# Last steps and end of a decoder layer redone: another drain order, norm and quantisation per token tile, FFN in two batches, rounding on GpSimd

## The reference, cut to what matters

```
x = x + ssm(layernorm(x))            # in projection, causal convolution, selective scan
                                     # with 128 heads in 8 groups, gate, group norm, out projection
x = x + matmul(fake_quant(layernorm(x), x1_scale, x1_zp),
               fake_quant(ctx, x2_scale, x2_zp))     # per sequence, 256 x 512 by 512 x 512
t = layernorm(x)[:, perm]            # FFN: features permuted
t = einsum('bhd,hdm->bhm', t, up)    # 16 heads, 32 -> 128
t = gelu(t)
t = einsum('bhm,hmd->bhd', t, down)  # 128 -> 32
x = x + t[:, unperm]
fake_quant(x, s, z) = (clip(round(x / s + z), 0, 255) - z) * s
```

## Time and profile before

| What | us |
|---|---|
| median of 3 runs (839.54 to 2028.73) | 841.23 |
| the profiled execution | 838.24 |
| its span in the trace | 836.4 |
| PE busy | 786.0 (94%) |
| VectorE (DVE) busy | 719.7 (86%) |
| GpSimd (POOL) busy | 589.6 (70%) |
| ScalarE (ACT) busy | 543.2 (65%) |
| share of PE in the chain that ended last | 88% |

### The profile page before, as it was taken

How to read it: one execution, slowest core, us unless ns; L and a number is a source line. 1 busy time by engine, 2 the same in 40 slices (tenths; PEclk the granted TensorE clock), 3 DMA queues, 4 the chain that set the end, 5 groups by cost and what they waited for, 6 DMA issues and landing times.

```text
span 836.4 us, 14376 instructions
## 1 busy us (share of the span) xinstructions
PE 786.0 (94%) x4212; PEld 613.4 (73%) x4212; DVE 719.7 (86%) x924; ACT 543.2 (65%) x1129; POOL 589.6 (70%) x487
## 2 busy tenths in 40 slices
PE   3765999999999999999999999999999989998987
PEld 2554777887787778777788878777888778776554
DVE  6767898999899989999898989898999999799663
ACT  2437677677667766776766776666677677885333
POOL 3436887778887877788787877887778877684100
PEclk9987999999999999999999999999999999999899
DMA  4253434444344344433434444433444444531001
GB/s 162 76 182 116 165 112 157 157 165 152 138 151 151 112 150 163 163 137 110 157 135 163 150 150 163 158 110 121 163 163 150 134 150 157 177 101 38 1 1 51
DMA packets 44049, 111.12 MB, mean 133 GB/s; under 512 B 5748, under 2 KB 6644, under 8 KB 44020
## 3 DMA queue, kind: packets, MB, share of 16 engines
q1 hardware_dynamic: 44020, 110.76, 38.5%
HBM read 109.30 MB, written 1.44 MB: 132 GB/s over the span
## 4 chain that ended last, share of the span: by engine, by line
PE 88%; DVE 5%; issue 3%; ACT 2%; POOL 1%; DMA 1%; SPq 0%; ACTq 0%; DVEq 0%; POOLq 0%
PE ps_in L1237 16%; PE ps_in L1239 15%; PE ps_in L1238 15%; PE ps_y L1348 7%; PE ps_o L1237 7%; PE ps_o L1239 7%; PE ps_o L1238 7%; PE ps_t L1310 3%; PE ps_y L1351 3%; PE ps_t L1322 1%; PE ps_o L1530 1%; POOL res L556 1%; PE ps_t L1360 1%; PE ps_o L1514 1%; DMA res<-in_x 1%
## 5 line engine op out<-in xcount | busy, mean ns | idle before, releaser
L510 POOL TENSOR_TENSOR w_lo<-raw,w_hi 128x512 fp32r<-128x512 f32 x144 | 231.5, 1629 | 135.7 <-ACT w_hi L625 126.5
L1237 PE MATMUL ps_in<-h_hi,w_hi 128*128 128x512 f32 x560 | 226.0, 404 | 0.0
L1239 PE MATMUL ps_in<-h_hi,w_lo 128*128 128x512 f32 x560 | 219.2, 392 | 0.0
L1238 PE MATMUL ps_in<-h_lo,w_hi 128*128 128x512 f32 x560 | 217.8, 389 | 0.0
L680 ACT ACTIVATE e<-e,nag 128x256 f32<-128x256 f32 (+1 forms) x512 | 183.5, 444 | 6.4 <-POOL e L530 6.4
L948 DVE SCALAR_TENSOR_TENSOR hid<-ps_in,curc,hid 128x510 f32<-128x510 f32 x186 | 138.3, 743 | 5.9 <-ACT hid L645 1.5
L1237 PEld LDWEIGHTS ps_in<-h_hi,w_hi 128*128 128x128 f32 x560 | 105.0, 187 | 30.2 <-issue 10.6
L645 ACT ACTIVATE hid<-ps_in,curc 128x512 f32<-128x512 f32 x62 | 48.2, 777 | 116.1 <-PE ps_in L1239 116.1
L1239 PEld LDWEIGHTS ps_in<-h_hi,w_lo 128*128 128x128 f32 x560 | 105.1, 188 | 23.4
L1238 PEld LDWEIGHTS ps_in<-h_lo,w_hi 128*128 128x128 f32 x560 | 105.3, 188 | 20.4
L541 POOL TENSOR_TENSOR e<-e,gm 128x512 f32<-128x512 f32 x64 | 100.9, 1576 | 25.1 <-DVE gm L990 25.0
(11 more groups left out here) (234 smaller groups left out, 1240.6 us busy)
## 6 DMA issues: line engine op xcount, KB each, us to landing
e<-acs_rows SPq DMA_DIRECT2D x64, 768.0 KB, 4.5
raw<-in_w_in SPq DMA_DIRECT2D x144, 256.0 KB, 4.7
rawo<-in_w_out SPq DMA_DIRECT2D x64, 256.0 KB, 4.0
craw<-in_ctx SPq DMA_DIRECT2D x8, 256.0 KB, 2.6
res<-in_x SPq DMA_DIRECT2D x4, 256.0 KB, 3.2
out_x<-res SPq DMA_DIRECT2D x4, 256.0 KB, 2.2
acs_rows<-z SPq DMA_DIRECT2D x3, 128.0 KB, 2.9
rawo<-in_w_dt SPq DMA_DIRECT2D x1, 256.0 KB, 4.9
```

The costliest lines, as they stand in the source:

```text
L510: pool.tensor_tensor(w_lo[:, slot, :], raw[:, slot, :], w_hi[:, slot, :].bitcast(F32), ALU.subtract).then_inc(s_lo, 1)
L1237: pe.matmul(dst, lh, rh, start=first, stop=False)
L1238: pe.matmul(dst, lh, rl, start=False, stop=False)
L1239: return pe.matmul(dst, ll, rh, start=False, stop=last)
```

## The change

Nothing is changed ahead of the last group of heads.

- The context tiles are rounded by GpSimd in place of VectorE, in the last group's steps behind `mask_rows`, the last one in the drain.
- Drain: ScalarE does the gate tanh of a tile ahead of the exponentials, and the last gate tanh ahead of the last context scale and keep and of the split of `up`; VectorE gates the last tile ahead of all `one_hot`; the token sums stand ahead of the last but one output tile; GpSimd's group root stands ahead of the low half of `up`.
- Norm and quantisation go per token tile: variance, power, scale and offset of one tile at a time. The scale comes out of the power by itself (the variance is multiplied by the squared quantisation scale first). Rounding is one operation, and the turned tile is float, made bf16 by ScalarE with a bias (`keep_turned`).
- 6 fillers stay of 38. The column products stand in two pairs.
- From the product on the two sequences are separate batches: features, take, up, down and put back in halves of 256 tokens, with the second batch's norm and product between the first one's steps. High halves of the down product are ScalarE's. The row terms are added in the last operation (`finish`) in place of four by ScalarE.
- The table for Gelu is loaded behind the first split of features.

Most removed lines of the stages behind the drain stand in the functions printed above and are left out here, as are helpers that repeat the form of another.

```diff
-WARM_A, WARM_B = 18, 20
+WARM_A = 6
...
-        q1 = e_flat[:, 4:6, :].rearrange("p a n -> p (a n)").bitcast(BF16).rearrange("p (t d) -> p t d", t=TT)
...
+        def turn_bank(t):
+            return feature_bank((t + 2) % TT)
+        def batch_bank(b, h):
+            return feature_bank((2 * b + h + 2) % TT)
+        def in_batch(a, b, h):
+            return a[:, 2 * h:2 * h + 2, b * SEQ:(b + 1) * SEQ]
+        def two(bank):
+            return bank.rearrange("p (k n) -> p k n", k=2)
+        def unit_of(b, kk, jj):
+            return 4 * b + 2 * kk + jj
...
+            def context_round(c):
+                pool.wait_ge(s_cs, c + 1)
+                pool.tensor_scalar(craw[:, c % 2, :], craw[:, c % 2, :], 255.0, MAGIC, ALU.min, ALU.add).then_inc(s_cc, 1)
...
+                if is_last(n) and t >= 1:
+                    context_round(t - 1)
...
             decays_off(last_m, CT - 1)
+            add_square(last_m, CT - 2)
             split_out(last_m, CT - 1)
-            add_square(last_m, CT - 2)
+            context_round(CT - 1)
+            group_rms(last_m)
             pool.wait_ge(s_uph, 1)
             pool.tensor_tensor(up_lo, up_raw, up_hi.bitcast(F32), ALU.subtract).then_inc(s_upl, 1)
-            group_rms(last_m)
-            for k, tiles in enumerate((slice(0, 2), slice(2, 4), slice(0, 2), slice(2, 4))):
-                pool.wait_ge(s_ev, k + 1)
-                pool.tensor_tensor(rstd[:, tiles], rstd[:, tiles], half[:, 0, tiles], ALU.pow).then_inc(s_ep, 1)
+            for k, dst in enumerate((qa, rstd)):
+                for t in range(TT):
+                    pool.wait_ge(s_ev, TT * k + t + 1)
+                    pool.tensor_tensor(dst[:, t:t + 1], rstd[:, t:t + 1], half[:, 0, t:t + 1], ALU.pow).then_inc(s_ep, 1)
...
             last_m = GROUPS - 1
+            gate_tanh(last_m, CT - 2)
             exps(last_m, CT - 1)
-            gate_tanh(last_m, CT - 2)
-            context_scale(CT - 1)
             context_keep(CT - 2)
             cast_out(last_m, CT - 2)
             z_high_and_square(last_m, CT - 2)
+            gate_tanh(last_m, CT - 1)
             cast_out(last_m, CT - 1)
+            context_scale(CT - 1)
+            z_high_and_square(last_m, CT - 1)
             context_keep(CT - 1)
-            gate_tanh(last_m, CT - 1)
             act.wait_ge(s_ffw, 32)
             act.wait_ge(s_in, NIN * GROUPS)
             act.activation(up_hi, up_raw, ACT.Copy).then_inc(s_uph, 1)
-            z_high_and_square(last_m, CT - 1)
-            act.preload_act_table(ACT.Gelu)
...
+            def keep_turned(t):
+                act.wait_ge(s_q1t, t + 1)
+                act.activation(q1T[:, t // 2, :, (t % 2) * P:(t % 2 + 1) * P],
+                               turn_bank(t).rearrange("p (k n) -> p k n", k=DK), ACT.Identity, bias=offset[:, :])\
+                   .then_inc(s_q1a, 1)
+            def feature_high(b, h):
+                act.wait_ge(s_ft, b + 1)
+                act.activation(in_batch(f_hi, b, h), two(batch_bank(b, h)), ACT.Copy).then_inc(s_fhi, 1)
...
+            def gelu(u):
+                act.wait_ge(s_up, u + 1)
+                act.activation(gel[u], up_banks(u), ACT.Gelu).then_inc(s_gl, 1)
...
-                act.activation(res[:, t, :], res[:, t, :], ACT.Identity, bias=rowq[:, t:t + 1]).then_inc(s_late, 1)
...
+            norm_scale(0)
+            norm_scale(1)
+            keep_turned(0)
+            norm_scale(2)
+            keep_turned(1)
+            norm_scale(3)
+            keep_turned(2)
+            keep_turned(3)
+            feature_high(0, 0)
+            feature_high(0, 1)
+            act.preload_act_table(ACT.Gelu)
+            permuted_high(0, 0)
+            permuted_high(0, 1)
+            gelu(0)
+            gelu(1)
+            feature_high(1, 0)
+            feature_high(1, 1)
+            gelu(2)
+            down_high(0, 0)
+            permuted_high(1, 0)
+            gelu(3)
+            permuted_high(1, 1)
+            gelu(4)
+            gelu(5)
+            down_high(0, 1)
+            gelu(6)
+            gelu(7)
+            down_high(1, 0)
+            down_high(1, 1)
...
-            context_round(CT - 1)
             gated(last_m, CT - 1)
+            skip_and_gate(last_m, CT - 1)
             one_hot(0)
...
+            one_hot(1)
+            one_hot(2)
             z_low(last_m, CT - 1)
...
             mean_square(last_m)
...
+            one_hot(3)
+            def variance(t, eps, scale):
                 dve.wait_ge(s_v, chain[0])
...
+                step_of(dve.bn_aggr(mv[:, t, :], stats[:, t, :]))
+                dve.tensor_scalar(rstd[:, t:t + 1], mv[:, t, 1:2], eps, scale, ALU.add,
+                                  ALU.bypass if scale is None else ALU.mult).then_inc(s_ev, 1)
             def statistics(t):
                 dve.bn_stats(stats[:, t, :], res[:, t, :]).then_inc(s_v, 1)
                 chain[0] += 1
...
+            def quant_variance(t):
+                variance(t, EPS, qd[:, 0:1])
+                step_of(dve.tensor_scalar(negm[:, t:t + 1], mv[:, t, 0:1], -1.0, None, ALU.mult))
+            def quant_offset(t):
+                dve.wait_ge(s_ep, t + 1)
+                dve.scalar_tensor_tensor(qb[:, t:t + 1], qa[:, t:t + 1], negm[:, t:t + 1], qs[:, 1:2],
+                                         ALU.mult, ALU.add).then_inc(s_aff, 1)
             def round_norm(t):
                 dve.wait_ge(s_x1, t + 1)
...
+                dve.tensor_scalar(e1[:, t, :], e1[:, t, :], 255.0, MAGIC, ALU.min, ALU.add).then_inc(s_q1, 1)
...
             def normalise(t):
...
+                dve.wait_ge(s_ep, TT + t + 1)
+                dve.wait_ge(s_q1t, t + 1)
                 dve.tensor_scalar(e1[:, t, :], res[:, t, :], mv[:, t, 0:1], rstd[:, t:t + 1],
                                   ALU.subtract, ALU.mult).then_inc(s_f, 1)
+            def row_terms(b):
+                dve.wait_ge(s_rs, b + 1)
+                dve.tensor_scalar(rowq[:, 2 * b:2 * b + 2], ps_in[:, 1 - b, 0:2], qd[:, 6:7], qd[:, 7:8],
+                                  ALU.subtract, ALU.mult).then_inc(s_rq, 1)
+            def feature_low(b, h):
+                dve.wait_ge(s_fhi, 2 * b + h + 1)
+                dve.tensor_tensor(in_batch(f_lo, b, h), two(batch_bank(b, h)), in_batch(f_hi, b, h).bitcast(F32),
+                                  ALU.subtract).then_inc(s_flo, 1)
...
+            def finish(t):
+                dve.wait_ge(s_fin, t + 1)
+                dve.wait_ge(s_rq, t // 2 + 1)
+                dve.scalar_tensor_tensor(res[:, t, :], turn_bank(t), rowq[:, t:t + 1], res[:, t, :],
+                                         ALU.add, ALU.add).then_inc(s_store, 1)
             dve.wait_ge(s_r, GROUPS)
...
+            dve.wait_ge(s_oin, 1)
+            add_output(0)
+            add_output(1)
+            first_statistics(0)
+            first_statistics(1)
+            quant_variance(0)
+            quant_variance(1)
+            dve.wait_ge(s_ou, STEPS)
+            add_output(2)
+            quant_offset(0)
+            first_statistics(2)
+            quant_offset(1)
+            quant_variance(2)
             round_norm(0)
+            add_output(3)
             round_norm(1)
...
+            quant_offset(2)
+            first_statistics(3)
+            quant_variance(3)
             round_norm(2)
+            add_product(0)
+            quant_offset(3)
+            last_statistics(0)
+            add_product(1)
+            variance(0, EPS, None)
+            last_statistics(1)
+            variance(1, EPS, None)
             round_norm(3)
...
+            normalise(0)
+            row_terms(0)
+            normalise(1)
             add_product(2)
...
+            feature_low(0, 0)
+            feature_low(0, 1)
             add_product(3)
...
+            last_statistics(2)
+            last_statistics(3)
+            variance(2, EPS, None)
+            permuted_low(0, 0)
+            variance(3, EPS, None)
             normalise(2)
+            row_terms(1)
             normalise(3)
...
+            permuted_low(0, 1)
+            feature_low(1, 0)
+            feature_low(1, 1)
+            down_low(0, 0)
+            permuted_low(1, 0)
+            permuted_low(1, 1)
+            down_low(0, 1)
+            finish(0)
+            down_low(1, 0)
+            finish(1)
+            down_low(1, 1)
+            finish(2)
+            finish(3)
...
             out_tile(last_m, CT - 3)
+            last_token_sums()
             out_tile(last_m, CT - 2)
-            last_token_sums()
...
+            def column_product(b):
+                for t in (2 * b, 2 * b + 1):
+                    pe.wait_ge(s_of, TT * last_m + t + 1)
+                    pe.matmul(out_bank(t), negrow[:, :], colrow[:, b, :], start=True, stop=False,
+                              skip_group_check=True)
+            def turn_rounded(t):
+                pe.wait_ge(s_q1, t + 1)
+                if t == TT - 1:
+                    pe.wait_ge(s_rq, 1)
```

(111 more changed lines are left out.)

208 lines of the change are left out of this document (33 added, 175 removed).

## The result

The changed kernel's median is 831.6 us (4 runs, 830.64 to 832.91) against 840.69 for the kernel before, measured beside it; the ratio is 0.9897, with a 95% interval of 0.9873 to 0.9921. The profiled execution lasted 830.81 us, with a span of 829.0.

A forecast was written before the change was run, and what follows sets the result against it. TensorE, busy 94% of the span, was taken as the bound. Terms -2.4 - 5.7 - 4.3 + 2.3, +2.6 for spells and -1.1 gave -8.6: 838.24 to 829.6, plus 2 for run spread, 831.7 us (829 to 834).

The forecast's parts named there:

- ten steps (rounding on GpSimd): Last group of heads: context rounding takes 0.9 us on GpSimd, free up to about 1.9 a step; 0, bounds -1 and +2.
- drain to first addition: Drain up to the first output addition: it comes at 776.7 instead of 779.09, 2.4 us earlier at full clock.
- first addition to first product: Norm and quantisation behind the drain: 7.7 us instead of 13.4, saving 5.7, or 4.7 with VectorE late by 1.
- first product to first take: From first product to the FFN's start: 9.2 us instead of 13.5, two tiles sufficing; 4.3 saved.
- FFN: From first take to the end: 28.7 us in halves against 26.4 before, one wait of 1.7 included; 2.3 lost.
- correction of the hand-overs: Whole tail: the same hand-overs put the kernel before 1.1 us too late, so 1.1 was taken off.
- The three late stages: First addition to product, product to take, and FFN: -5.7, -4.3 and +2.3 us.
- Rival D: Last group's steps: GpSimd's rounding is a slow form, deciding from about 2 us each; at 5 us, 857; chance 0.04.
- One sign of being wrong: Last group: the prediction is wrong if GpSimd's splits start to hold TensorE; no size given.
- The clock: Tail: two spells at half clock, each 3.4 us long and costing 1.3; +2.6 together.
- Rival A: Behind the drain: clock stays low without fillers, one to three more spells of 1.3 each, 833 to 836 us; chance 0.14.
- Rivals B and C: Behind the drain: B, VectorE bounds both middle stages, 835 us, 0.10; C, batch 1 holds back batch 0, 836, 0.06.

The follow-up runs named there:

- end_order: Changed kernel with the last down half ahead of the second put back and the last split ahead of the second finish; 827.76 us, ratio 0.9857.
- after_again: The changed kernel itself, unedited, measured a second time beside a version without fillers; 831.83 us, ratio 0.9885.
- full_fill: Changed kernel with the FFN over all 512 tokens at once and twenty fillers ahead of the turning of the features; 838.07 us, ratio 0.9984.
- full_width: Changed kernel with the FFN over all 512 tokens at once instead of in batches, without those twenty fillers; 840.24 us, ratio 0.9980.
- sums_between: Changed kernel with the token sums spread, two behind each of out tile 6's four token tiles; 830.74 us, ratio 0.9882.

## Why the prediction was right, and where it was not

The forecast's terms against the profiled execution, before to after, in us:

| term | predicted | measured |
|---|---|---|
| ten steps (rounding on GpSimd) | 0 | +2.1 |
| drain to first addition | -2.4, +1.3 for a spell | -1.1 |
| first addition to first product | -5.7 | -5.6 |
| first product to first take | -4.3, +1.3 for a spell | -4.2 |
| FFN | +2.3 | +2.3 |
| behind the last matmul (3.2 for 3.9) | 0 | -0.7 |
| start of the ten steps | 0 | -0.3 |
| correction of the hand-overs | -1.1 | none |
| sum (of the spans: 829.0 less 836.4) | -8.6 | -7.4 |

**The three late stages** came out as worked out, each within 0.1 us: one turned tile's copy 0.68 (0.75 taken), the rounding of the norm 0.45, the half take and the up units by TensorE's spacing, one wait of 1.45 before the third put back (1.7 taken). They could be summed because each is a chain of instructions that have rows in the trace before, and TensorE and VectorE were both followed.

**The drain** was under-valued by its own terms and then hit by chance. With no half-clock stretch it takes 18.8 us from the last transposes (three kernels with the rounding on VectorE, one with it on GpSimd) where the sum had 19.5 (776.7 less 757.23). The token sums start 12.5 us behind the last transposes in all four, and the sum had 13.5 (770.7): it moved the sums by the 4.3 us of the gate tanh alone, but from that tanh to the sums it is 5.0 us in end_order, where it was 5.9 in the kernel before. Between the two VectorE built the first one_hot (1.9 us, from 770.27 to 772.12); the prediction named its move behind the last gating and gave it no price. The stretch in the drain cost 1.6, not 1.3 (20.36 in after_again, 18.75 in end_order). In the first profile of the changed kernel another 0.4 us lie ahead of the token sums, of which more below.

**The step that failed is the rounding on GpSimd**: "I take 0.9" was 2.08 us. A one-input instruction with two operations isn't near the select's 0.69; it is above the two-input subtract's 1.60, outside both bounds. At 2.08 the ten steps are 109.2 to 109.7 us in nine profiles against 107.4 to 107.5 in four with VectorE. Rival D, a slow form whose place is the last group's steps, is thus right in kind: it put the point of decision at 2 us each. The rule beside the price, that up to 1.9 us a step cost nothing, would have given 7 x 0.18 = 1.3 of the 2 us lost; the rest is that idle time summed over a stage isn't free time at each point. The idle time of the last four steps was 7.3 us and the four roundings there took 9.1. No run has a rounding of 0.9 us on GpSimd, so the rule is untested at the price that the prediction took. One sign of being wrong came true but for its letter: GpSimd did hold TensorE in the last group (the four waits in end_order), not by its splits but by the decays that stand in its queue behind the roundings. The Trainium skill ("GPSIMD Engine Reference", section "Engine selection") has one-input operations roughly at line rate; here the same instruction took 2083 ns on GpSimd and 574 on VectorE, and the measurement decides.

In the profiled execution of the changed kernel this loss is disguised. At 676 to 679 a half-clock stretch lengthens one step from 12.55 to 14.1 us, ahead of the first rounding at 687.9, and the later steps are shorter by 1.3 (72.2 for 73.5 in end_order): 109.6 in all with that stretch, 109.4 without it (after_again, end_order). I first read it as a loss by the clock that had nothing to do with the change. Ten steps and drain together are 130.4 us in the four profiles that have both this stretch and one in the drain (the changed kernel, the two without fillers, full_fill) and 129.7 to 129.8 in the two that have only the one in the drain (after_again, full_width), so the early stretch costs 0.7. No profile with the rounding on VectorE has such an early stretch; among the profiles without one it is 109.2 to 109.4 against 107.4 to 107.5, and that difference is the rounding's.

**The clock**: two spells were counted and two came, but only the one in the drain stood where the prediction had it. The other came at 676, ahead of all that it looked at, and none came behind the column products; that the number fits is chance. A stretch lay in the drain in 9 of the 14 profiles, and up to three more stood at other places: behind the column sums, between products and first take, in the FFN. Rival A is not dead: after_again had two behind the first addition. What speaks for its mechanism is full_width, where the clock was at 0.50 for 9.2 us through waits, row sums and sixteen transposes; twenty fillers ahead of the same transposes kept it at 1.00. The Trainium skill ("TensorE: Matmul & The Clock Gate", section "PE-mode transpose") says that transposes don't count as activity for the clock. Full_width agrees with that and is no proof, since TensorE also stood idle there for 3.6 of the 9.2 us; the changed kernel's 51 us at 1.00, with transposes between short bursts, show that they need not bring the clock down.

Rivals B and C fell: TensorE waited 0.33 us for a rounding of VectorE's at 787.16 and 0.98 for its split before the first take, and batch 1 never held back batch 0's take halves. The errors (rounding +2.1, no spell on the way to the take -1.3, last stores -0.7, start -0.3, hand-overs +1.1, roundings of the terms) cancel to 1.2: the profiled execution was to last 829.6 us and lasted 830.81. The 2 us added for the spread of the runs were 1.2 too much, since the median lies 0.8 above the profiled execution. The two errors cancel, so a forecast that hits to 0.1 us is luck; what the prediction earned are the three late stages.

## What to carry to other kernels

Before an operation is moved to an engine with idle time, look for a row of that very form on that engine; where there is none, the nearest rows bound it badly, and the idle time has to lie in the queue where the instruction is put. Where runs differ by more than the effect, cut the profiles into stages and compare these: two edits of 2 us each were plain there and could be added up with confidence. Having cut a stage into batches, look at which product stands in front of each wait: exchanging two won 1.9 us here.

## What was not expected of the hardware

- A one-input two-operation instruction on a 128x512 float tile took 1.92 to 2.47 us on GpSimd (eight of them) and 0.41 to 0.42 on VectorE (six of the eight roundings of the kernel before). The other two took 1.51 and 1.52 us: each began 0.1 to 0.5 us after a two-input instruction of GpSimd's and ended 0.3 us after that one ended. Four of the six overlapped GpSimd's work too, but had begun first, and were not slowed.
- Half-clock stretches of about 3.4 us wander: the same kernel had them at 676 and 775 in one execution and at 775, 789 and 795 in another. With the sparse work ahead of one taken away (sums_between) there was none in the drain but two behind it, and other versions had none in the drain with that work in place.
- What half-clock stretches cost went by what the stage waited for: one cost 0.7 us in the ten steps and the drain together, with GpSimd late anyway (130.4 against 129.7), one 1.6 in the drain (20.36 against 18.75), two together 2.4 before the first take.
